# State-space phase: normed rows one batch ahead, inner products in the first pairs, softplus input earlier, row writes later

## The chip, the cores and the metric

The kernel runs on one core of one Trainium2 chip. The metric is the device time of one execution in microseconds, lower is better. The core's engines run their own instruction streams in order and meet through semaphores: PE (TensorE, matrix products; PEld are its weight loads), DVE (VectorE), ACT (ScalarE, functions from loaded tables), POOL (GpSimd), and SP, which issues transfers. TensorE's clock has two levels, 1.2 and 2.4 GHz; the profile gives the granted clock as a share of the full one.

## The reference

A two-layer decoder with residual blocks on x of shape (16, 256, 128). The change is in the first block only, which computes for each of the 16 sequences of 256 rows:

```python
xr = xn @ in_proj_w.T                       # xn: layer norm, then rms norm
xm, res = split(xr, 2)                      # 256 + 256 columns
u = silu(conv1d(xm, 4 taps) + conv_b)
dt, Bm, Cm = split(u @ x_proj_w.T, [8, 24]) # 8, 16 and 16 columns
delta = softplus(dt @ dt_proj_w.T + dt_proj_b)
h = exp(delta * A) * h + delta * Bm * u     # a scan over 256 rows, 16 states per channel
y = (einsum(h, Cm) + u * D) * silu(res)
x2 = rmsnorm(y @ out_proj_w.T + xn)         # then 8 experts, the best 2 for each row
```

Cross attention, a quantised feed-forward, and a second layer of the same kind of blocks follow; nothing in them changes.

## The kernel before, in words

`mamba` (L233) is one block with five instruction streams. Each of the 16 batches is one sequence of 256 rows (two groups of 128), and t counts the batches. The 16 states are taken in NP = 8 pairs p, and for each pair DVE does one scan for each half c of the 256 channels (L964) and then multiplies the states by the C rows (L973).

What a batch needs, in the order of the data:

- POOL `front` (L395): reciprocal deviations and scale factors of the rows. ACT `norm_in` (L503) makes h, ACT `unit` (L511) makes xn, PE `turn_in` (L743) turns xn into PSUM, ACT `turn_in` (L556) copies it to xnT. POOL `grow` (L426) adds h to the residual.
- PE `conv_in` (L751), twice, and `res_in` (L764): the in-projection with the four taps folded in, and the gate branch. ACT `front` (L561): silu of both, waiting first for the two convolutions and then for the gate branch.
- PE `dbl_out` (L772): the inner products that give dt, B and C. ACT `steps_out` (L571) copies them. PE `pre_out` (L782): dt to the width of delta.
- ACT `soft` (L580): softplus as max(x, 0) + log(1 + exp(-abs(x))): absolute value, exponential em, positive part. POOL `lost_part` (L418): the rounding that 1 + em loses. ACT `logarithm` (L594). POOL `steps_in` (L430): delta and du = delta * u. PE `turn_du` (L789), ACT `duT_in` (L620).
- `weigh` on three engines makes du * B for the states: POOL (L408) every even state, ACT (L598) the odd states of even pairs, DVE (L1017) the odd states of odd pairs. PE `feed` (L696) turns them into the scan's input. ACT `decays` (L608) makes exp(delta * A) of a pair.
- PE `spread` (L712) spreads the C rows of a pair over the partitions, `sums` (L733) adds the products, DVE `gate` (L975) multiplies with silu(res). PE `turn_y` (L798), ACT `yT_in` (L627), PE `carry` and `out` (L844, L807): the out-projection. ACT `size_out`, `store` (L520, L527), PE `turn_rows`, `gates` (L815, L825), ACT `rows_in`, `gates_in` (L535, L541): the normed output row and its gate logits. In batches 6, 10 and 14 DVE chooses experts (`choose`), and PE's `ranks` and DVE's `slots` follow in the next one; POOL's `sets` (L464) sends finished rows with indirect transfers from batch 7 on.

The order of work is written out by hand. Each engine has its own loop over t (POOL L473, ACT L642, PE L864, DVE L1028), and work for batch t + 1, and for the output of t - 1 and t - 2, stands between the pairs of batch t. PE does, for each pair p: a feed of pair p + 1, sums of p - 1, spread of p, sums, the second feed, and then what the loop lists for that p. xmP holds in turn the convolution, dt with B and C, softplus's input, and du turned; resP holds in turn xn turned, the gate branch, and y turned.

## Time and profile before

| | us |
|---|---|
| three timed runs | 2945.87, 2952.32, 2958.49 (median 2952.32) |
| the profiled execution | 2946.31, its span 2944.6 |
| PE busy in the span | 2435.7 (83%) |
| DVE busy | 1889.2 (64%) |
| ACT busy | 1669.0 (57%) |
| POOL busy | 1042.4 (35%) |
| state-space phase, scans of L964 | from 46.4, the last starts at 680.0 |
| granted clock over the span | 0.902 |

The span is one execution from its first to its last instruction. A row of the timeline is a run of like instructions of one engine with its start, its length, and in brackets how long the engine idled before it and who released it; a run overlaps the next one slightly, since instructions are pipelined. The share of busy time is a mean over phases with different limits.

### The profile page before, as it was taken

What the parts mean: (1) busy time and instruction counts of PE and PEld (TensorE: products, weight loads), DVE (VectorE), ACT (ScalarE), POOL (GpSimd) and SP (SyncE); (2) the same over time, 40 slices, a digit from 0 to 9 for tenths busy, and PEclk for the clock granted to TensorE, in tenths of its full rate; (3) what the DMA queues carried; (4) which work ended last, traced back from release to release, by engine and by line L of the source; (5) the groups of instructions that cost most, each with busy time, mean ns of one, the idle gap of its engine ahead of it and who ended that gap; (6) DMA issues with size and microseconds to landing.
All of it is one profiled execution on the core that took longest, in us unless ns stands there. A gap on an engine that the chain in (4) does not pass through costs nothing. (4 is left out here: it accounts for less than half of the span.)

```text
span 2944.6 us, 51871 instructions
## 1 busy us (share of the span) xinstructions
PE 2435.7 (83%) x17357; PEld 1874.4 (64%) x17359; DVE 1889.2 (64%) x3977; ACT 1669.0 (57%) x4651; POOL 1042.4 (35%) x1579
## 2 busy tenths in 40 slices
PE   5888788873995999998964896999998769989396
PEld 4777777763993666665642774666665547756385
DVE  5888777773224766666779453777776447767355
ACT  5777777771223777764554343877875346645011
POOL 4455564644451111102221312222220155523654
PEclk8998988886996999998985987999998979999598
DMA  8400000002652000000002100000000000000266
GB/s 344 191 1 1 8 8 5 12 1 89 192 174 73 2 1 1 2 1 7 1 8 47 24 1 18 1 1 2 1 2 9 9 9 1 1 9 14 88 204 198
DMA packets 73992, 130.00 MB, mean 44 GB/s; under 512 B 29113, under 2 KB 47361, under 8 KB 69634
## 3 DMA queue, kind: packets, MB, share of 16 engines
q1 hardware_dynamic: 62210, 103.46, 11.4%
q0 software_dynamic: 9216, 19.02, 1.8%
q10 hardware_dynamic: 2304, 4.20, 0.4%
q8 instruction: 143, 2.34, 0.3%
q14 instruction: 119, 0.97, 0.1%
HBM read 69.23 MB, written 57.41 MB: 43 GB/s over the span
## 5 line engine op out<-in xcount | busy, mean ns | idle before, releaser
L964 DVE TENSOR_TENSOR_SCAN s_state<-s_decay,s_inP 128x512 f32<-128x512 f32 x256 | 297.2, 1201 | 28.6 <-PE s_inP L708 15.3
L1890 ACT ACTIVATE s5a_prob<-s5a_scoreP,s5a_nmax 128x256 f32<-128x256 f32 x512 | 236.0, 482 | 22.6 <-DVE s5a_nmax L2070 21.0
L1890 ACT ACTIVATE s2s_prob<-s2s_scoreP,s2s_nmax 128x128 f32<-128x128 f32 (+1 forms) x512 | 208.6, 425 | 41.5 <-DVE s2s_nmax L2068 39.1
L708 PE MATMUL s_inP<-ident,s_wb 128*128 128x128 f32 x1024 | 174.3, 306 | 67.5 <-POOL s_wb L415 52.2
L617 ACT ACTIVATE s_decay<-s_delta,s_aneg 128x255 f32<-128x255 f32 x512 | 216.5, 496 | 3.7 <-POOL s_delta L434 3.4
L3651 POOL DMA_INDIRECT parts<-m_y,m_to x160 | 153.1, 957 | 134.6 <-DVE m_y L3742 109.5
L2070 DVE TENSOR_REDUCE s5a_nmax<-s5a_scoreP 128x4 f32<-128x1024 f32 x128 | 156.2, 1220 | 67.0 <-PE s5a_scoreP L1991 64.7
L708 PEld LDWEIGHTS s_inP<-ident,s_wb 128*128 128x128 f32 x1024 | 139.1, 161 | 78.7 <-issue 56.4
L973 DVE TENSOR_TENSOR s_state<-s_state,s_cP 128x512 f32<-128x512 f32 x256 | 162.0, 673 | 37.5 <-PE s_cP L720 37.5
L739 PE MATMUL s_ysumP<-ident,s_state 128*128 128x128 f32 x1024 | 164.7, 286 | 17.4 <-DVE s_state L973 17.4
L2068 DVE TENSOR_REDUCE s2s_nmax<-s2s_scoreP 128x2 f32<-128x256 f32 (+1 forms) x256 | 130.0, 550 | 76.1 <-PE s2s_scoreP L1986 73.6
L2081 DVE TENSOR_TENSOR s5a_probT<-s5a_probP,s5a_mask 128x768 f32<-128x768 f32 x128 | 122.5, 957 | 62.8 <-PE s5a_probP L2001 61.7
L2079 DVE COPY s2s_probT<-s2s_probP 128x768 f32<-128x768 f32 x128 | 122.6, 957 | 53.1 <-PE s2s_probP L2001 53.0
L3840 PE MATMUL m_hidP<-m_xT,m_w 128*128 128x256 f32 x640 | 155.3, 387 | 0.0
L1991 PE MATMUL s5a_scoreP<-s5a_k,s5a_q 32*128 32x256 f32 x1024 | 146.8, 404 | 0.8 <-ACT s5a_k L1870 0.8
L739 PEld LDWEIGHTS s_ysumP<-ident,s_state 128*128 128x128 f32 x1024 | 128.4, 149 | 22.1 <-DVE s_state L973 22.1
L415 POOL TENSOR_TENSOR s_wb<-s_duT,s_bct 128x512 f32<-128x512 f32 x128 | 132.1, 1060 | 15.7 <-ACT s_duT L625 15.3
L3840 PEld LDWEIGHTS m_hidP<-m_xT,m_w 128*128 128x128 f32 x640 | 118.2, 195 | 13.3
L3848 PEld LDWEIGHTS m_yP<-m_w,m_act 128*128 128x128 f32 x960 | 119.5, 192 | 4.7 <-DVE m_act L3734 0.7
L3848 PE MATMUL m_yP<-m_w,m_act 128*128 128x128 f32 x960 | 120.0, 275 | 0.5 <-DVE m_act L3734 0.5
L1986 PE MATMUL s2s_scoreP<-s2s_k,s2s_q 32*128 32x128 f32 (+1 forms) x1024 | 119.7, 352 | 0.0
L3798 ACT ACTIVATE m_act<-m_hidP 128x1024 f32<-128x1024 f32 x40 | 41.0, 1025 | 132.3 <-PE m_hidP L3840 132.3
(647 smaller groups left out, 6339.1 us busy)
## 6 DMA issues: line engine op xcount, KB each, us to landing
sorted<-blank SPq DMA_DIRECT2D x32, 1105.0 KB, 28.4
m_w<-in_m_w SPq DMA_DIRECT2D x40, 512.0 KB, 4.1
m_w<-in_m_w SPq DMA_DIRECT2D x40, 384.0 KB, 3.7
m_xin<-sorted SPq DMA_DIRECT2D x80, 130.0 KB, 2.5
m_back<-parts SPq DMA_DIRECT2D x16, 256.0 KB, 6.6
m_back<-parts ACTq DMA_DIRECT2D x16, 256.0 KB, 7.3
s4w_mats<-s_scratch SPq DMA_DIRECT2D x4, 1024.0 KB, 12.6
parts<-m_y,m_to POOLq DMA_INDIRECT x160, 3.3
```

The source lines that it names most:

```text
L415: ins = nc.gpsimd.tensor_tensor(wb[:, n, :, :], duT[:], bct[s][:, :, n:n + 1].to_broadcast([P, TB, 256]), ALU.mult)
L617: ins = nc.scalar.activation(decay[c][:, n, 1:], delta[:, c, 1:], ACT.Exp, scale=aneg[:, c, n:n + 1])
L708: ins = nc.tensor.transpose(inP[i % 3][:, a, g * P:(g + 1) * P], wb[:, k // 2 * 2 + a, g, c * P:(c + 1) * P], ident[:])
L739: ins = nc.tensor.matmul(ysumP[:, g, c * P:(c + 1) * P], state[r][:, c, a, g * P:(g + 1) * P], ident[:], start=False, stop=(p == NP - 1 an ...
L964: nc.vector.tensor_tensor_scan(flat(state[i % RING][:, c]), flat(decay[c][:, 2 * p:2 * p + 2, :]), flat(inP[(2 * i + c) % 3][:]), 0.0, ALU ...
L973: nc.vector.tensor_tensor(part, part, cP[:], ALU.mult).then_inc(S["prodded"], 1)
L1890: ins = nc.scalar.activation(prob[i][:, h, a:b], scoreP[i][:, h, a:b], ACT.Exp, bias=nmax[:, p % 4, h, r:r + 1], accum_out=den[s][:, r, 2 ...
L1991: ins = nc.tensor.matmul(scoreP[i][:, h, a:b], q[rows_of(h), c, r * P:r * P + P], k[rows_of(h), c, :], start=True, stop=True)
L2070: ins = nc.vector.tensor_reduce(nmax[:, p % 4, :, :].rearrange("p h r -> p (h r)"), scoreP[i][:].rearrange("p h (r k) -> p (h r) k", r=2), ...
L3651: nc.gpsimd.indirect_dma_start(acc, bass.IndirectOffsetOnAxis(to[s][:, i:i + 1], 0), y[s][:, i, :], None).then_inc(put[s], 16)
L3840: ins = nc.tensor.matmul(hidP[s % 2][:, c, :], w1[s][:, c, :], xT[s % 2][:], start=True, stop=True)
L3848: ins = nc.tensor.matmul(yP[s % 2][:, i * C:i * C + C], act[s % 2][:, k, i * P:i * P + P], w2[s][:, k, :], start=(k == 0), stop=(k == HK - 1))
```

## The change

It changes the order of the hand-written streams, a ring of buffers and two waits. Every operation of a batch stays, in number and size.

- The ring xn has 4 buffers where it had 3. ACT makes h and xn two batches ahead (in batch t for t + 2) and PE turns them then, after pair 5. Before, it was one batch ahead, in pairs 0 to 2.
- PE's convolutions of t + 1 stand behind pairs 0 and 1 (before 1 and 2), the gate branch and inner products behind 2 (before 3), the product for delta behind 3 (before 4), y's turning behind 3 (before 1), the rows' turning behind 6 (before 5).
- ACT's silu block stands behind the exponentials of pair 2 (before 5), the copy of dt, B and C behind the weighing for pair 4, softplus's first part behind the weighing for pair 6 (before behind the exponentials of pair 6). Row writes and the copy of y come after it.
- POOL's `front` stands behind its third weighing (before its eighth), and the addition of h, two of the row sends and the lost part stand between the eighth and delta.

```diff
-        xn = [sc.sb(f"xn{r}", [P, TB, C]) for r in range(3)]
+        xn = [sc.sb(f"xn{r}", [P, TB, C]) for r in range(4)]
             lost_part(0)
+            grow(1)
             steps_in(0, 0)
...
-                for p in range(4):
-                    weigh(t, s, p)
-                if more:
-                    grow(t + 1)
-                for p in range(4, 6):
-                    weigh(t, s, p)
-                if lot is not None and k < 3:
-                    sets(lot, 3 * k, 3 * k + 2)
-                for p in range(6, NP):
+                for p in range(3):
                     weigh(t, s, p)
                 if t + 2 < NB:
                     front(t + 2)
+                for p in range(3, NP):
+                    weigh(t, s, p)
                 if more:
                     lost_part(t + 1)
+                if t + 2 < NB:
+                    grow(t + 2)
+                if lot is not None and k < 3:
+                    sets(lot, 3 * k, 3 * k + 2)
+                if more:
                     steps_in(t + 1, 1 - s)
...
             def unit(t, s):
-                wait(ac, S["kept"], t - 2)
+                wait(ac, S["kept"], t - 3)
...
             soft(0)
+            norm_in(1)
+            unit(1, 1)
             logarithm(0)
+            turn_in(1)
             for t in range(NB):
                 decays(t, 0)
                 duT_in(t)
                 weigh(t, s, 0)
-                if more:
-                    norm_in(t + 1)
                 decays(t, 1)
-                if more:
-                    unit(t + 1, 1 - s)
                 weigh(t, s, 2)
                 decays(t, 2)
                 if more:
-                    turn_in(t + 1)
+                    front(t + 1, 1 - s)
                 decays(t, 3)
                 weigh(t, s, 4)
+                if more:
+                    steps_out(t + 1, 1 - s)
+                decays(t, 4)
+                weigh(t, s, 6)
+                if more:
+                    soft(t + 1)
                 if t >= 2:
                     store(t - 2)
                 if t >= 1:
                     yT_in(t - 1)
-                decays(t, 4)
-                weigh(t, s, 6)
                 decays(t, 5)
-                if more:
-                    front(t + 1, 1 - s)
-                    steps_out(t + 1, 1 - s)
+                if t + 2 < NB:
+                    norm_in(t + 2)
+                    unit(t + 2, s)
                 decays(t, 6)
                 if t >= 1:
                     size_out(t - 1)
-                if more:
-                    soft(t + 1)
+                if t + 2 < NB:
+                    turn_in(t + 2)
                 decays(t, 7)
...
             def res_in(t, s):
-                wait(pe, S["yT_ready"], t - 1)
+                wait(pe, S["yT_ready"], t - 2)
...
             def turn_y(t, above):
-                pe.wait_ge(S["xnT_ready"], above + 1)
+                pe.wait_ge(S["sres_ready"], above + 1)
...
                     if p == 0:
                         if more:
-                            turn_in(t + 1, 1 - s)
+                            conv_in(t + 1, 1 - s, 0)
                         skip(t, s)
...
                     elif p == 1:
                         if more:
-                            conv_in(t + 1, 1 - s, 0)
-                        if t > 0:
-                            turn_y(t - 1, min(t + 1, NB - 1))
+                            conv_in(t + 1, 1 - s, 1)
                     elif p == 2:
-                        if more:
-                            conv_in(t + 1, 1 - s, 1)
-                    elif p == 3:
                         if more:
                             res_in(t + 1, 1 - s)
                             dbl_out(t + 1, 1 - s)
-                    elif p == 4:
+                    elif p == 3:
                         if more:
                             pre_out(t + 1, 1 - s)
+                        if t > 0:
+                            turn_y(t - 1, min(t + 1, NB - 1))
+                    elif p == 4:
                         if t > 0:
                             carry(t - 1, 1 - s)
                             out(t - 1)
                     elif p == 5:
+                        if t + 2 < NB:
+                            turn_in(t + 2, s)
+                    elif p == 6:
                         if t >= 2:
                             turn_rows(t - 2)
```

## Rows read from the trace of the kernel before

**Rows 1.** Groups, 45 to 685 us: line, engine, tiles, count; busy, mean ns; idle before.

```profile
L964 DVE TENSOR_TENSOR_SCAN s_state<-s_decay,s_inP 128x512 f32<-128x512 f32 x256 | 297.2, 1201 | 28.6 <-PE s_inP L708 15.3 <-ACT s_decay L617 13.2
...
L973 DVE TENSOR_TENSOR s_state<-s_state,s_cP 128x512 f32<-128x512 f32 x256 | 162.0, 673 | 37.5 <-PE s_cP L720 37.5
...
L1024 DVE TENSOR_SCALAR s_wb<-s_duT,s_bct 128x256 f32<-128x256 f32 x127 | 53.8, 464 | 33.5 <-ACT s_duT L625 33.5
...
L980 DVE TENSOR_TENSOR s_yg<-s_ysumP,s_sres 128x512 f32<-128x512 f32 x16 | 11.1, 692 | 22.7 <-PE s_ysumP L739 22.7
```

**Rows 2.** Timeline of DVE, batch 5: start, length, line, tiles, count [idle before].

```profile
231.67 1.40 DVE L1024 TENSOR_SCALAR s_wb<-s_duT,s_bct 128x256 f32<-128x256 f32 x2 [1.82 <-ACT s_duT L625]
...
238.41 0.69 DVE L980 TENSOR_TENSOR s_yg<-s_ysumP,s_sres 128x512 f32<-128x512 f32 x1 [1.84 <-PE s_ysumP L739]
...
248.36 2.32 DVE L964 TENSOR_TENSOR_SCAN s_state<-s_decay,s_inP 128x512 f32<-128x512 f32 x2
...
255.47 1.28 DVE L973 TENSOR_TENSOR s_state<-s_state,s_cP 128x512 f32<-128x512 f32 x2 [1.37 <-PE s_cP L720]
...
260.25 1.29 DVE L973 TENSOR_TENSOR s_state<-s_state,s_cP 128x512 f32<-128x512 f32 x2 [0.72 <-PE s_cP L720]
```

**Rows 3.** Timeline of ACT, batch 5.

```profile
232.49 0.86 ACT L507 ACTIVATE s_h<-xres,s_shift,s_n_rstd 128x128 f32<-128x128 f32 x2
...
234.85 0.68 ACT L517 ACTIVATE s_xn<-s_h,s_rr 128x128 f32<-128x128 f32 x2
...
239.68 1.69 ACT L617 ACTIVATE s_decay<-s_delta,s_aneg 128x255 f32<-128x255 f32 x4
241.27 0.90 ACT L605 ACTIVATE s_wb<-s_duT,s_bct 128x256 f32<-128x256 f32 x2
...
245.12 0.60 ACT L631 ACTIVATE s_yT<-s_resP 128x512 f32<-128x512 f32 x1 [2.45 <-PE s_resP L804]
...
249.71 1.28 ACT L565 ACT_TABLE_LOAD   x1
251.01 0.84 ACT L565 ACTIVATE s_u<-s_xmP,s_convb 128x256 f32<-128x256 f32 x2
252.09 0.60 ACT L569 ACTIVATE s_sres<-s_resP 128x512 f32<-128x512 f32 x1 [0.24 <-PE s_resP L768]
...
259.38 0.84 ACT L586 ACTIVATE s_mag<-s_xmP,s_dtb 128x256 f32<-128x256 f32 x2
...
264.78 0.63 ACT L596 ACTIVATE s_lg<-s_em 128x512 f32<-128x512 f32 x1
...
269.58 0.57 ACT L625 ACTIVATE s_duT<-s_xmP 128x512 f32<-128x512 f32 x1
```

**Rows 4.** Timeline of PE, batch 5.

```profile
233.02 2.79 PE L708 MATMUL s_inP<-ident,s_wb 128*128 128x128 f32 x12 [2.42 <-POOL s_wb L415]
...
239.20 1.12 PE L729 MATMUL s_ysumP<-s_dd,s_u 128*128 128x128 f32 x8
...
242.27 0.66 PE L708 MATMUL s_inP<-ident,s_wb 128*128 128x128 f32 x4 [0.21 <-DVE s_state L964]
...
247.11 1.90 PE L759 MATMUL s_xmP<-s_xnT,s_wtap 128*128 128x256 f32 x8
...
251.02 1.03 PE L768 MATMUL s_resP<-s_win,s_xnT 128*128 128x256 f32 x4
...
256.17 1.12 PE L786 MATMUL s_xmP<-s_dtT,s_dtw 8*128 8x256 f32 x4
...
268.50 0.63 PE L795 MATMUL s_xmP<-ident,s_du 128*128 128x128 f32 x4 [2.06 <-POOL s_du L437]
```

**Rows 5.** Timeline of POOL, the end of batch 5.

```profile
265.74 1.26 POOL L434 TENSOR_TENSOR s_delta<-s_pos,s_lg 128x512 f32<-128x512 f32 x1
```

**Rows 6.** Stretches: length, busy us of PE, PEld, DVE, ACT, POOL, granted clock, transfers.

```profile
231.70:240.00 8.30, 6.98 (x37) 6.97 (x38) 5.29 (x7) 6.82 (x18) 8.28 (x9) 0.59 0.01 3
...
284.00:288.00 4.00, 4.00 (x18) 3.42 (x17) 4.00 (x5) 0.01 (x1) 0.00 (x0) 0.66 0.00 0
```

**Rows 7.** Timeline of PE, the first lull of batch 6.

```profile
283.64 1.11 PE L708 MATMUL s_inP<-ident,s_wb 128*128 128x128 f32 x4 [3.21 <-DVE s_state L964]
```

More of the change, by code:

```diff
@@ L514, in unit @@
                 wait(ac, S["turned"], t - 1)
-                wait(ac, S["kept"], t - 2)
+                wait(ac, S["kept"], t - 3)
                 for g in range(TB):
-                    ins = nc.scalar.activation(xn[t % 3][:, g, :], h[:, g, :], ACT.Copy, scale=rr[:, g:g + 1])
+                    ins = nc.scalar.activation(xn[t % 4][:, g, :], h[:, g, :], ACT.Copy, scale=rr[:, g:g + 1])
                 ins.then_inc(S["xn_ready"], 1)
@@ L747, in turn_in @@
                 for g in range(TB):
-                    ins = nc.tensor.transpose(turnP[:, g * P:(g + 1) * P], xn[t % 3][:, g, :], ident[:])
+                    ins = nc.tensor.transpose(turnP[:, g * P:(g + 1) * P], xn[t % 4][:, g, :], ident[:])
                 ins.then_inc(S["turned"], 1)
@@ L850, in carry @@
                 for g in range(TB):
-                    ins = nc.tensor.matmul(outP[:, g, :], ident[:], xn[t % 3][:, g, :], start=(g == 0), stop=False)
+                    ins = nc.tensor.matmul(outP[:, g, :], ident[:], xn[t % 4][:, g, :], start=(g == 0), stop=False)
                 ins.then_inc(S["kept"], 1)
@@ L859, in _ @@
             pre_out(0, 0)
+            turn_in(1, 1)
             turn_du(0)
```

## The prediction

> **What bounds the kernel now.** The change touches only the state-space phase, some 46 to 681 us of the span, 16 batches of about 38.5 us in a plain one. I read first the groups of that stretch with the idle time before each [rows 1]: DVE carries the recurrence (16 scans a batch), and what it idles for are outputs that wait for PE's spread C rows (37.5 us in all) and, once a batch, the first weighing, which waits for ACT's copy of duT (33.5 us). The scans and the gate add 28.6 and 22.7 us. So a batch is DVE's work plus about 7 us of idle. Then I read one plain batch, number 5, in order of time on each engine. Its zero is 231.63, where ACT has copied duT (the second such copy, 269.58 + 0.57, gives a period of 38.5) [rows 2, 3]. DVE idles 1.82 there, 1.2 before the first scan, 1.84 before the gate, and in the middle 1.37 and 0.72, where PE comes late with the spread of pairs 4 and 5 [rows 2]. ACT is far ahead in the middle: the exponentials of pair 3 run at 239.68, and their scan starts at 248.36 [rows 2, 3]. PE is the tight engine of the first pairs: its feed at 242.27 waited 0.21 us only [rows 4]. That reserve of ACT, some 7 us, is what the new order spends.
>
> **The change, part by part.** Nothing is computed that was not computed before; instructions change places. Times below are microseconds after the zero of the batch.
>
> *PE's first pairs.* The first convolution (8 matmuls; the group at 247.11 has 1.90, of which about 0.17 overlaps the next group: 1.73) moves from pair 1 to pair 0 and takes the place of the turning of xn (0.22, the skip products follow at 239.20) [rows 4]. So PE reaches the feed in front of the second convolution about 1.3 us later (1.5 less the 0.21 of waiting): the convolution in pair 1 starts at 12.4 and not 11.1, and ends at 14.1. Pair 2 then runs feed, sums, spread, sums, feed, five groups of 0.43, to 16.3. DVE's pair 1 is not late: its spread ends at 11.5, and its scans end at about 11.6.
>
> *ACT's front.* It stood after the exponentials of pair 5 and now stands before those of pair 3, as one block: silu of u, silu of the gate branch, and the next exponential needs its table back. The table for silu (1.28) is loaded while ACT waits. The gate branch is copied 1.07 after the start of its product (251.02 to 252.09) [rows 3, 4], so at 17.4. The copy takes 0.5, the table 1.30 (249.71 to 251.01 shows the step) [rows 3]: the exponentials start at 19.2, the first two are done at 20.0. DVE was ready for the scan of pair 3 at 16.7 [rows 2]. That is a new idle of about 3.2 us where there was none.
>
> The Trainium skill's ScalarE: Activation LUTs, section What ACT_TABLE_LOAD costs, asks about 2.66 us for each change of table, a drain included. The row has 1.28 and the next activation 0.02 behind it, so the trace does not show that drain here, and the sum goes by the row; by the page this one step would be 1.4 us a batch dearer.
>
> *The feed behind it.* ACT's weighing for pair 4 follows the exponentials of pair 3 (1.6, then 0.9) and is done at 21.7. Before, it was done at 10.5 (241.27) [rows 3]. PE's feed of pair 4 waits for it at the head of pair 3. Behind that feed are queued the sums of pair 2 and the spread of pair 3, on which DVE's outputs of pair 3 wait. PE is through with the gate product and the inner products at 19.1 (three groups like the 1.03 at 251.02, less their overlaps: 2.8), so it idles 2.6 us. The spread ends at 23.0; DVE's scans of pair 3 end at 22.3, so it idles 0.7 more. Then PE has the product that widens dt (1.05, the group at 256.17) at 23.9 to 24.9 [rows 4]. In the old order it ended at 25.6, so softplus's input comes only 0.7 us earlier, not a pair earlier.
>
> *From softplus to the next batch on ACT.* In the new order everything between is a chain without waits: softplus 2.1 (259.38 and what follows it), yT 0.5, exponentials of pair 5 1.6, h and xn 0.8 + 0.6, pair 6 1.6, pair 7 1.6, table 1.3, logarithm 0.6 [rows 3], and four small ones (row write, sizes, xnT, rowT), which I price by the copy of yT and below it, 0.45 each: 12.5 us, so the logarithm is done at 37.4. It was done at 33.8 (264.78 + 0.63 less the zero). DVE, let go at pair 5 by its exponentials (28.9, the end of its first two), does scans and outputs 5, 6 and 7 at 3.45 each and ends at 39.3. From the logarithm the tail is the old one: delta and du on POOL 1.3 each, turning 0.7, duT 0.6 with hops: 4.0, so 41.4. POOL's three steps of the lost part, 4.6 us, leave this tail, but they ended only some 0.2 us behind the logarithm (delta starts at 265.74, the logarithm ends at 265.41) [rows 3, 5], so moving them is worth 0.2 us at the most. The new wait of y's turning (for the gate branch's silu, done at 17.9) is met when PE comes to it at 24.9, and the turning of xn at 31.2 finds xn made at 31.1. Row writes and the turnings on PE count nothing beyond the chain above, since DVE is still busy; if not, each costs its own 0.2 to 0.6.
>
> *Sum without a change of clock.* Period 41.4 against 38.5: +2.9. Check by DVE's idle: +3.2 and +0.7 new; 1.37 and 0.72 gone, for which 0.3 and 0.6 come back (pair 4 behind the moved turning of y, pair 5 behind its exponentials); boundary 1.8 to 2.1; this gives +3.0. Plain batches 0 to 5: 6 x 2.9 = 17.4. Batches 6, 10 and 14 have the choice of experts on DVE (4 us), which hides the new ACT wait: +0.2 each. Batches 7 and 11 put the rank products (some 2 us of PE) into pair 0 beside the moved convolution, where there is no backlog to spare, and start with a clock that rises a little sooner: +3.5 each. Batches 8, 9, 12 and 13: 2.9 plus 0.25, because POOL's sends stand between du and the next weighing: 12.6. Batch 15 has no next batch: 0. The prologue has POOL's addition of h (0.7) before delta. Together 17.4 + 0.6 + 7.0 + 12.6 + 0.7 = 38 us.
>
> *PE's clock.* The new 2.6 us lull comes in the middle of busy PE. Before, the lull of 3.21 us before 283.64 was followed by a granted clock of 0.66 for 284 to 288 (part of it at the lower level, 1.2 of 2.4 GHz), and four transposes took 1.11 there, 0.66 at 242.27 [rows 4, 6, 7]. Two more batches with a choice show lulls of 3.3 to 3.5 us. At the batch's start, where the lulls are 2.06 and 2.42 us with 0.6 of work between (the first at 268.50, the second at 233.02; one such pair at each of the plain starts), the stretch 231.7 to 240 has 0.59 [rows 4, 6]. So 2.6 us alone is between a case that always falls and gaps of 1 us that never do; I take it to fall in about two batches of three. Price: PE is the critical engine from the feed to the product for delta (3.4 us of work at the full level, twice that at the lower). A short fall, as at 283.64, costs half its length of 3.4 us, 1.7; a long one, as at the starts, the whole 3.0; mean 2.1 us. Bounds: nothing in 15 batches, or 3.0 in all, 45 us. Value: ten to fourteen batches x 2.1, I take 26.
>
> The Trainium skill's TensorE: Matmul & The Clock Gate, section HAM oscillation — how this bites in real kernels, describes a wait of PE that returns in every iteration and lets the clock fall each time; by it all 15 batches would pay, about 31 us for my 26.
>
> The profiled execution took 2946.3 us (span 2944.6), at the low end of the three timed ones (2945.9 to 2958.5, median 2952.3). Its own time plus 38 plus 26 is 3010 us. I leave it there; measured from the median it would be 6 us more.
>
> **The rivals.**
> *A, the clock holds.* The same new waits, no fall: 2946 + 38 = 2984. For it: 2.6 us is shorter than the 3.21 that fell. Against: the pair of lulls at each start falls every time.
> *B, faster: the relief of pairs 4 and 5 decides.* If ACT gets its front's inputs before DVE needs pair 3, only the removal of PE's late spreads stays: 2.09 us x 15 = 31, so 2915. It decides at the time of the gate product: it would have to start by 13.0 (DVE's 16.7 less 1.07, 0.5, 1.3 and 0.85 for the first two exponentials), and it stands behind a feed that needs the first scan of pair 2, which DVE finishes at 14.0, and 0.43 for the feed. So even a PE with no backlog misses it by 1.4 us; only a shorter hop or table would help.
> *C, the waits only change places.* What pair 3 costs, pairs 4 and 5 and the tail give back, if the chain from softplus had slack that I do not see (2.9 us): 2950.
> *D, every lull falls long.* 2946 + 38 + 45 = 3029. The longer boundary lull (about 2.9 before the turning of du where it was 2.06) [rows 4] speaks for it.
>
> **How the numbers follow.** Forecast 0.58 (own range 2992 to 3024), A 0.22, D 0.06, B 0.08, C 0.06. The predicted time is 3010. The range runs from A's lower side to D, 2970 to 3034, and leaves out B, C and a little at the top. What this kernel's measurement can tell is about 0.5%, 15 us. Slower by more: forecast, A, D = 0.86; B gives faster 0.08, C within 0.06.
>
> **What would show it.** Right: DVE's scans of pair 3 wait about 3 us for ACT's exponentials in each of batches 0 to 5; ACT idles some 7 us before its first silu; PE idles about 2.6 us before the feed of pair 4, released by ACT's weighing; four transposes behind it take about 1.1 us; POOL's part step no longer stands before delta; a plain period is 41 to 44 us. Wrong: a period of 38.5 or less; silu of the gate branch finished before 16; a clock of 1.0 behind the lull (then A); a logarithm done before 36.

## The result and the profile after

The changed kernel takes 3033.73 us (3021.62 to 3042.58) beside 2951.79 for the kernel before: ratio 1.027, 95% interval 1.022 to 1.033. One of its four runs (3071.77, granted clock 0.879) fell in a slower state that some executions of any kernel here show, and the medians and ratios of this document leave such runs out. The change is slower, as forecast, by 24 us more than the 3010 named; the time lies inside the range of 2970 to 3034, by less than 1 us. The execution profiled is the longest of the three (3042.58): its span is 3040.8 us, 96 more than before.

Where the 96 us lie is read from the first and last load of m_xin, with which the expert phase begins and ends. The first one is issued at 733.8 us before and at 819.9 after: the state-space phase, with what is left of it behind the last batch, costs 86 us. From the first to the last load it is 2164.2 before and 2174.6 after, though nothing there was changed. The twelve profiles of the experiments scatter there: 2161.6 to 2173.4 in x1 to x7, 2183.5 to 2194.9 in x8 to x12, whose executions of before were also some 30 to 40 us longer. So I count these 10 us as no part of the change, and below I compare the ends of the state-space phase ("phase end", always the first load of m_xin) beside the ratios.

The groups of the changed kernel from 45 to 785 us (line, engine, tiles, count, busy, mean ns, idle before):

```profile
L969 DVE TENSOR_TENSOR_SCAN s_state<-s_decay,s_inP 128x512 f32<-128x512 f32 x256 | 297.3, 1201 | 61.3 <-ACT s_decay L617 46.9 <-PE s_inP L711 14.3
...
L978 DVE TENSOR_TENSOR s_state<-s_state,s_cP 128x512 f32<-128x512 f32 x256 | 161.9, 672 | 57.5 <-PE s_cP L723 57.4
...
L1029 DVE TENSOR_SCALAR s_wb<-s_duT,s_bct 128x256 f32<-128x256 f32 x128 | 83.3, 691 | 49.6 <-ACT s_duT L625 49.6
```

Against [rows 1] DVE's scans have the same 1201 ns, but DVE idles 33 us more ahead of them, all of it for ACT's exponentials. Ahead of the outputs it idles 20 more, and the weighings themselves are 30 us dearer (691 ns for 464). The wait ahead of the first weighing of each batch has hardly grown: of the 49.6 us, 13.8 are the wait of the very first one, which begins at 44.73 and is not among the 127 of [rows 1], so that like for like it is 35.9 for 33.5. So some 50 us of the loss are waits, and 30 are longer weighings.

Batch 5 of the changed kernel begins at 261.47 (duT copied), and the next at 307.05: 45.6 us for 38.5. DVE in it (start, length, line, tiles, count, idle before):

```profile
269.59 2.26 DVE L1029 TENSOR_SCALAR s_wb<-s_duT,s_bct 128x256 f32<-128x256 f32 x2
...
278.61 0.60 DVE L1029 TENSOR_SCALAR s_wb<-s_duT,s_bct 128x256 f32<-128x256 f32 x2
281.35 2.33 DVE L969 TENSOR_TENSOR_SCAN s_state<-s_decay,s_inP 128x512 f32<-128x512 f32 x2 [2.14 <-ACT s_decay L617]
284.87 1.28 DVE L978 TENSOR_TENSOR s_state<-s_state,s_cP 128x512 f32<-128x512 f32 x2 [1.19 <-PE s_cP L723]
...
292.18 1.28 DVE L978 TENSOR_TENSOR s_state<-s_state,s_cP 128x512 f32<-128x512 f32 x2 [3.79 <-PE s_cP L723]
...
307.08 1.40 DVE L1029 TENSOR_SCALAR s_wb<-s_duT,s_bct 128x256 f32<-128x256 f32 x2 [1.82 <-ACT s_duT L625]
```

ACT in the same batch:

```profile
266.41 1.28 ACT L565 ACT_TABLE_LOAD   x1
275.46 0.84 ACT L565 ACTIVATE s_u<-s_xmP,s_convb 128x256 f32<-128x256 f32 x2 [7.76 <-PE s_xmP L762]
278.51 0.60 ACT L569 ACTIVATE s_sres<-s_resP 128x512 f32<-128x512 f32 x1 [2.21 <-PE s_resP L771]
279.12 1.28 ACT L617 ACT_TABLE_LOAD   x1
280.42 1.70 ACT L617 ACTIVATE s_decay<-s_delta,s_aneg 128x255 f32<-128x255 f32 x4
282.02 0.89 ACT L605 ACTIVATE s_wb<-s_duT,s_bct 128x256 f32<-128x256 f32 x2
...
288.51 0.84 ACT L586 ACTIVATE s_mag<-s_xmP,s_dtb 128x256 f32<-128x256 f32 x2 [2.84 <-PE s_xmP L789]
...
302.22 0.63 ACT L596 ACTIVATE s_lg<-s_em 128x512 f32<-128x512 f32 x1
```

And PE, with the granted clock of stretches of 4 us behind it (length, busy of PE, PEld, DVE, ACT, POOL, clock, transfers):

```profile
277.44 1.03 PE L771 MATMUL s_resP<-s_win,s_xnT 128*128 128x256 f32 x4
...
279.36 1.08 PE L781 MATMUL s_xmP<-s_xp_bc,s_u 128*128 128x32 f32 x8
283.06 0.63 PE L711 MATMUL s_inP<-ident,s_wb 128*128 128x128 f32 x4 [2.62 <-ACT s_wb L605]
...
286.40 2.07 PE L789 MATMUL s_xmP<-s_dtT,s_dtw 8*128 8x256 f32 x4
```

```profile
280.00:284.00 4.00, 1.38 (x13) 1.30 (x13) 2.33 (x2) 3.99 (x12) 0.00 (x0) 1.00 0.00 0
284.00:288.00 4.00, 4.00 (x18) 3.23 (x15) 3.13 (x4) 1.67 (x5) 0.00 (x0) 0.53 0.01 4
288.00:292.00 4.00, 4.00 (x19) 3.60 (x18) 0.40 (x1) 3.46 (x9) 1.90 (x1) 0.50 0.00 0
292.00:296.00 4.00, 4.00 (x28) 4.00 (x27) 3.82 (x5) 3.92 (x12) 3.45 (x4) 0.69 0.00 0
```

These rows show one event spread over three engines. ACT waits for the convolution and for the gate product (7.76 and 2.21), changes its table, and only then has the exponentials for which DVE stands 2.14. PE stands 2.62 for ACT's weighing. A few instructions later the granted clock is at its lower level, 1.2 of 2.4 GHz, and stays there for about 10 us. In them the product that widens dt takes 2.07 where it took 1.12 in [rows 4], and DVE stands 3.79 for the spread of pair 4.

### The profile page after: what moved, and what is told of

It is laid out like the page before. It is cut to its first block and busy times, and to the rows that moved or that the text cites. A ratio compares the mean times of both kernels' runs of the same rounds, so it can differ in the third digit from the quotient of the medians.

```text
span 3040.8 us, 51871 instructions
## 1 busy us (share of the span) xinstructions
PE 2490.7 (82%) x17359; PEld 1909.6 (63%) x17359; DVE 1924.2 (63%) x3977; ACT 1668.6 (55%) x4651; POOL 1045.3 (34%) x1579
## 5 line engine op out<-in xcount | busy, mean ns | idle before, releaser
L969 DVE TENSOR_TENSOR_SCAN s_state<-s_decay,s_inP 128x512 f32<-128x512 f32 x256 | 297.3, 1201 | 61.3 <-ACT s_decay L617 46.9
L711 PE MATMUL s_inP<-ident,s_wb 128*128 128x128 f32 x1024 | 185.6, 320 | 107.6 <-POOL s_wb L415 47.6
L742 PE MATMUL s_ysumP<-ident,s_state 128*128 128x128 f32 x1024 | 175.3, 299 | 14.9 <-DVE s_state L978 14.9
L742 PEld LDWEIGHTS s_ysumP<-ident,s_state 128*128 128x128 f32 x1024 | 137.2, 157 | 21.2 <-DVE s_state L978 21.2
L415 POOL TENSOR_TENSOR s_wb<-s_duT,s_bct 128x512 f32<-128x512 f32 x128 | 132.9, 1070 | 15.1 <-ACT s_duT L625 13.8
L421 POOL TENSOR_SCALAR s_part<-s_em 128x512 f32<-128x512 f32 x16 | 31.0, 1939 | 269.3 <-ACT s_em L589 269.3
```

What stands on the lines that cost most here:

```text
L415: ins = nc.gpsimd.tensor_tensor(wb[:, n, :, :], duT[:], bct[s][:, :, n:n + 1].to_broadcast([P, TB, 256]), ALU.mult)
L711: ins = nc.tensor.transpose(inP[i % 3][:, a, g * P:(g + 1) * P], wb[:, k // 2 * 2 + a, g, c * P:(c + 1) * P], ident[:])
L742: ins = nc.tensor.matmul(ysumP[:, g, c * P:(c + 1) * P], state[r][:, c, a, g * P:(g + 1) * P], ident[:], start=False, stop=(p == NP - 1 an ...
L969: nc.vector.tensor_tensor_scan(flat(state[i % RING][:, c]), flat(decay[c][:, 2 * p:2 * p + 2, :]), flat(inP[(2 * i + c) % 3][:]), 0.0, ALU ...
```

## The experiments

Two theories of the loss. **Theory 1:** ACT's block with both silus, put in front of pair 3's exponentials, is the cause: directly by its waits, and through the lull of PE and the lower clock behind it. **Theory 2:** POOL's new places are the cause: its scale factors for the batch after next stand between its third and fourth weighing, so that its later weighings run beside DVE's, its part of softplus stands beside another weighing of DVE's, and DVE's weighings are slowed. Five runs (x1 to x5) tell these apart, the other seven ask what bounds the batch once they are gone. Where single batches are compared, a batch is taken from one copy of duT to the next.

**x1, the silu block moved back by one pair.**

```
                 decays(t, 2)
-                if more:
-                    front(t + 1, 1 - s)
                 decays(t, 3)
                 weigh(t, s, 4)
                 if more:
+                    front(t + 1, 1 - s)
                     steps_out(t + 1, 1 - s)
```

> The changed kernel with one block moved on ACT: the silu block of the next batch stands behind the exponentials of pair 3 and the weighing for pair 4, not before them. Theory 1 (the place of this block starts the new waits, PE's lull of 2.6 us behind the inner products and the fall of the clock after it): DVE's scans of pair 3 no longer wait (2.14 us a batch in the changed kernel), PE's feed of pair 4 no longer waits 2.6 us, the clock no longer falls in mid batch; 15 batches x about 4 us less, so about 2975 us, and a plain batch of 39 to 41 us. Rival (PE's new order alone, the convolution in pair 0 and the turnings behind pairs 5 and 6, makes it slow): the time stays above 3020 us.

2970.54 us, ratio 1.0074 (1.0056 to 1.0093), phase end 752.0: 68 of the 86 us are gone with one block moved by four exponentials and a weighing. The granted clock no longer falls behind the inner products in any batch of its trace. DVE in x1:

```profile
247.22 1.80 DVE L1028 TENSOR_SCALAR s_wb<-s_duT,s_bct 128x256 f32<-128x256 f32 x2
...
266.04 2.33 DVE L968 TENSOR_TENSOR_SCAN s_state<-s_decay,s_inP 128x512 f32<-128x512 f32 x2 [1.20 <-ACT s_decay L617]
...
279.11 1.40 DVE L1028 TENSOR_SCALAR s_wb<-s_duT,s_bct 128x256 f32<-128x256 f32 x2 [2.73 <-ACT s_duT L625]
```

The weighing for pair 3 (247.22) still takes three times as long as the next one (0.60 at 255.77), and the wait at the end of the batch has grown from 1.82 to 2.73.

**x2, POOL's steps behind its eighth weighing, all else as changed.**

```
-                for p in range(3):
+                for p in range(NP):
                     weigh(t, s, p)
                 if t + 2 < NB:
                     front(t + 2)
-                for p in range(3, NP):
-                    weigh(t, s, p)
```

> The changed kernel with POOL's scale factors for t + 2 made behind its eighth weighing, as before the change, and not between the third and the fourth. Theory 2 (DVE's weighing for pair 3 takes 2.0 us in the changed kernel and not 0.6 to 0.8, because it now runs beside a POOL weighing, and that lengthens the batch by itself): 15 x 1.3 us less, about 3018 us. Theory 1: DVE waits for ACT two pairs later anyway, so the weighing gets short again but the time falls by 0 to 8 us, 3030 to 3038.

3034.22 us, 1.0292 (1.0279 to 1.0305), phase end 820.4: nothing in sum. In the plain batches 0 to 5 a shorter weighing ends in a longer wait, while DVE stands for ACT and PE further down the batch (0.5 us more in all six together). Batch by batch the sum hides two effects: batches 6 and 10 are 3.5 and 3.6 us shorter, and batches 8 and 12 are 3.7 and 3.8 longer, because in these two the granted clock now falls behind the lull of 2.62, which it did not in the changed kernel.

**x4, both moves** (the two diffs above together).

> The changed kernel with both moves of the first two experiments. Theory 1 with theory 2 as the next limit: without the wait for ACT, DVE paces the batch, and the shorter weighing for pair 3 counts in full: 10 to 19 us less than the move of the silu block alone, about 2960 us. If DVE does not pace it then (PE or ACT does): the same as with the silu block alone, within 5 us.

2953.85 us, 1.0022 (1.0011 to 1.0033), phase end 742.8. The same POOL move that was worth nothing in sum is now worth 9 us of phase (17 in the medians). The weighing that took 1.80 in x1 beside POOL's weighings, and what POOL does beside it now:

```profile
246.26 0.61 DVE L1026 TENSOR_SCALAR s_wb<-s_duT,s_bct 128x256 f32<-128x256 f32 x2
```

```profile
245.98 0.71 POOL L398 TENSOR_TENSOR s_n_rstd<-s_var,s_n_power 128x2 f32<-128x2 f32 x1
```

But the shorter weighing is not what pays most. Of the 9.8 us in the batches 7.6 lie in 6, 10 and 14, where DVE chooses experts. In the other twelve the weighings are 10.6 us shorter in all, and 7.1 us of that come back as waits ahead of the outputs, for PE's spread. In x1, as in the changed kernel, some steps of the choice run beside POOL's weighings and take four times as long; the first row is of the changed kernel, the second of x4:

```profile
315.34 0.97 DVE L1000 SCALAR_TENSOR_TENSOR s_conv<-s_conv,s_col 128x64 f32<-128x64 f32 x1
```

```profile
286.29 0.23 DVE L997 SCALAR_TENSOR_TENSOR s_conv<-s_conv,s_col 128x64 f32<-128x64 f32 x1
```

The whole choice takes 5.33 and 4.57 us in batches 6 and 10 of x1, and 3.66 and 3.74 in x4. PE's lull behind it shrinks with it, from 4.08 and 2.95 to 2.40 and 2.48, and the clock, which fell behind the lull in x1, holds. So theory 2's mechanism is real and a tenth of the loss, but most of it comes through the batches with a choice. The Trainium skill, SBUF — State Buffer, section Terms, says that DVE and GpSimd arbitrate for one pair of ports, and that an instruction holds it to its end. The rows agree in direction for the weighing (1.80 beside POOL's weighings, 0.61 beside its small scale-factor steps); DVE's scans keep their 1201 ns beside the same weighings.

**x3 and x5, the lull of PE filled.** x3 computes the products for B and C three times instead of once (32 columns wide, into the same place). x5 puts eight products without use, 128 wide, into a place that is written afterwards. x3, then x5:

```
+                for again in range(3):
+                    for g in range(TB):
+                        for c in range(2):
+                            ins = nc.tensor.matmul(bctP[:, g, :], ...)
```

```
                     nc.tensor.matmul(dtP, xp_dt[:, c, :], u[s][:, c, :], start=(c == 0), stop=(c == 1))
+                keep_busy(nc, xmP[:, 0, P:2 * P], ident, 8)
```

> The changed kernel with the B and C products of each batch computed three times over into the same place, so that PE works 1.8 us longer behind the inner products, in time in which it idled for 2.6 us. Nothing waits longer for it, since ACT copies them 1.8 us later at the earliest. If the lull lets the clock fall: the granted clock behind it stays at 1.0, four transposes there take 0.6 and not 1.06 us, and the time falls by the half of the 78 us of added low clock or a little less, 25 to 39 us, to about 3005. If the clock falls for another reason, or its fall costs nothing: 3038, or some us more.

> The changed kernel with eight products of the identity with itself (128 x 128, some 1.9 us) between the dt product and the B and C products, into a part of xmP that is not read. The third experiment filled the same lull with narrow products (32 columns), and the clock fell all the same behind a lull of 0.84 us. If narrow products keep the clock up less than wide ones: the granted clock stays at 1.0 behind the lull, and the time falls by 20 to 35 us below the 3026 us of the third experiment or, from the changed kernel's 3038, by 25 to 39. If what lies before the lull does not matter and 0.8 us of idle time is enough: 3025 as in the third experiment.

x3: 3026.7 us, 1.0262 (1.0246 to 1.0277), phase end 810.0. It missed: the lull was 0.84, and in batch 5 the clock fell all the same.

```profile
273.50 2.87 PE L782 MATMUL s_xmP<-s_xp_bc,s_u 128*128 128x32 f32 x24
277.20 0.63 PE L711 MATMUL s_inP<-ident,s_wb 128*128 128x128 f32 x4 [0.84 <-ACT s_wb L605]
277.67 0.88 PE L742 MATMUL s_ysumP<-ident,s_state 128*128 128x128 f32 x4
278.34 1.06 PE L723 MATMUL s_cP<-ident,s_bct 128*128 128x128 f32 x4
```

x5: 2998.82 us, 1.0155 (1.0109 to 1.0200), phase end 786.2. The lull is the same 0.83, and four transposes behind it take 0.60:

```profile
269.73 0.63 PE L711 MATMUL s_inP<-ident,s_wb 128*128 128x128 f32 x4 [0.83 <-ACT s_wb L605]
270.20 0.60 PE L742 MATMUL s_ysumP<-ident,s_state 128*128 128x128 f32 x4
```

The granted clock from 120 to 680 us: first the changed kernel, then x3, then x5 (before has 0.90).

```profile
120.00:680.00 560.00, 438.00 (x2843) 384.28 (x2841) 420.30 (x536) 374.75 (x857) 268.64 (x322) 0.85 0.02 5
```

```profile
120.00:680.00 560.00, 457.48 (x3083) 401.02 (x3084) 427.63 (x545) 383.96 (x881) 277.06 (x333) 0.88 0.02 5
```

```profile
120.00:680.00 560.00, 452.87 (x3192) 396.40 (x3192) 441.29 (x571) 388.73 (x892) 277.59 (x334) 0.92 0.02 5
```

So the clock is worth 34 us of phase end (35 of the medians). Nearly all of it (34.2 of 35.9 us in the batches) lies in the eleven batches in which the changed kernel's clock fell behind this lull, 3.1 us for each. With the narrow products the clock fell behind it in nine batches (it held in 2 and 3), with the wide ones in none. The wait for ACT's exponentials stays in x5 (2.15 in batch 5), as it should. The Trainium skill, TensorE: Matmul & The Clock Gate, section HAM oscillation — how this bites in real kernels, describes a kernel in which PE waits some 3 to 5 us in every iteration and the clock falls in each. Here the wait is shorter, 2.62 us, and the clock fell behind it in eleven batches of fifteen. In the batches 8, 9, 12 and 13 it held: the same lull of 2.62 stands before 429.37, and the transposes behind it take 0.60. The prediction read the page as if all 15 would pay.

**x6 and x7, the end of the batch.** x6 is the kernel before with three small moves on ACT: softplus ahead of the sums of squares, the logarithm ahead of the copy of the output row, and the gate logits of the batch one later. x7 has the second and third in x4, and there softplus behind the exponentials of pair 5. The edit of x6:

```
                 weigh(t, s, 0)
+                if t >= 3:
+                    gates_in(t - 3)
...
                 decays(t, 6)
-                if t >= 1:
-                    size_out(t - 1)
                 if more:
                     soft(t + 1)
+                if t >= 1:
+                    size_out(t - 1)
                 decays(t, 7)
-                if t >= 2:
-                    rows_in(t - 2)
                 if more:
                     logarithm(t + 1)
                 if t >= 2:
+                    rows_in(t - 2)
+                if t == NB - 1:
                     gates_in(t - 2)
```

> The kernel before, with three moves on ACT alone: softplus's first part before the squares of the output rows (which wait for PE's out-projection), the logarithm before the copy of the turned rows, and the copy of the gate logits one batch later, behind the first weighing. Theory (the tail from softplus's input through the logarithm, delta, du and duT sets the gap between two batches; the changed kernel moved em but left the logarithm behind the copy of the rows): em and the logarithm come 1.9 us earlier, DVE's wait of 1.82 us before its first weighing goes nearly to 0, 15 x 1.8 = 27 us less than before, about 2922. Rival (the tail is set elsewhere, by PE's turning of du behind the gate products or by the scan's feed): 2945 to 2952.

> The fourth experiment (silu block behind the weighing for pair 4, POOL's scale factors behind its eighth weighing) with four more moves on ACT: the exponentials of pair 5 before softplus's first part and behind the copy of y, the logarithm before the copy of the turned rows, and the copy of the gate logits one batch later. In the fourth experiment a batch still has 1.2 us of waiting for the exponentials of pair 5, 1.0 us of PE for the copy of y, and 2.7 us before the first weighing. Theory: 1.2 of the first and some 0.9 of the last go, 15 x 2.1 = 31 us less than the fourth experiment's 2955, about 2925. Rival (PE's load in pairs 0 to 2 with the clock at its lower level sets the batch): not below 2945.

x6: 2914.20 us, 0.9929 (0.9889 to 0.9969; the two medians alone give 0.988), phase end 699.2: faster than both kernels. DVE no longer stands at the end of a plain batch (5.8 us in all ahead of its weighings, for 33.5 in [rows 1]), its weighing starts on time (and is then 1.87 long, beside POOL's). Ahead of the scans and of the gate it idles 8 and 7 us less. In pair 4 it stands as before:

```profile
243.38 1.28 DVE L975 TENSOR_TENSOR s_state<-s_state,s_cP 128x512 f32<-128x512 f32 x2 [1.38 <-PE s_cP L722]
...
256.19 1.87 DVE L1026 TENSOR_SCALAR s_wb<-s_duT,s_bct 128x256 f32<-128x256 f32 x2
```

x7 missed: 2964.44 us, 1.0058 (1.0044 to 1.0072), phase end 751.0, worse than x4. The plain batches are a little better (2 to 5 take 156.3 us, 157.6 in x4), those from 7 on worse (43.9 for 41.4 in batch 7), for a reason that x9 shows below: in batches 7, 8, 9, 11, 12 and 13 delta starts 2.3 to 2.5 us behind the logarithm, behind POOL's row sends, and in all others 0.08. Batch 5 shows why the order of the small copies gains little there: from the table load in front of the exponentials of pair 4 (254.70) to the end of the logarithm (270.62) ACT never idles. It is 15.9 us of work in a row, in which the change has put h and xn of the batch after next (1.57) between softplus and the logarithm. That gave the third theory: **in the new order a plain batch is as long as ACT's chain.**

**x8 and x9, h and xn taken out of that chain.** x8 is x4, and x9 is x7, with

```
                 weigh(t, s, 4)
+                if t + 2 < NB:
+                    norm_in(t + 2)
+                    unit(t + 2, s)
                 if more:
                     front(t + 1, 1 - s)
...
                 decays(t, 5)
-                if t + 2 < NB:
-                    norm_in(t + 2)
-                    unit(t + 2, s)
```

and x10 is x6 again.

> This is x4_both_moves with one more move: ACT makes h and xn of the batch after next (s_h, s_xn; 1.57 us) in its wait for the convolution (5.26 us in the trace of x4), and no longer between softplus and the logarithm. Theory 1 (what keeps the new order slower than before is ACT's unbroken chain from the gate branch's silu to the logarithm, which the change made longer by the rows of the batch after next): the logarithm comes about 1.6 us earlier in each of 14 batches, the boundary wait of DVE falls from 2.7 to about 1.1, the time from 2955 to 2930 to 2936. Theory 2 (the boundary is held by something else, the turning of xn or the gates on PE's queue ahead of du, or POOL): unchanged, 2950 to 2958.

> This is x7_change_repaired with the same one move (s_h and s_xn before the silu block). Theory 1: the chain is shorter by 1.6 us, and the waits of x7 at scan 6 (0.88) and most of the boundary's 2.75 go with it; 2964 becomes 2938 to 2944 if x7's 9 us above x4 stay, 2925 to 2932 if the wait at scan 6 was their cause. Theory 2: unchanged, 2960 to 2966.

> x6_before_tail_shorter again, on the same chip as the two others, to compare with them: 2912 to 2922, 1% faster than before. If its gain was chance, 2945 to 2955.

Beside these three the kernel before took 2977.94 us, so only ratios are compared: x8 1.0014 (1.0000 to 1.0027), x9 1.0006 (0.9994 to 1.0018), x10 0.9900 (0.9868 to 0.9932). x10 confirms x6. x8 and x9 gained less than expected (0.1% on x4, which is not clear of the intervals, and 0.5% on x7). In x9 the plain batches did what the theory says: four of them (2 to 5) take 149.9 us, 156.3 in x7 and 153.8 before, so 1.6 us less for each. In x8 they take 155.2 for 157.6 in x4, 0.6 each where 1.6 was expected, and DVE's wait at the end of batch 5 fell from 2.72 to 1.82 and not to 1.1: ACT now stands 0.81 for PE's turning of the row in front of the logarithm. What failed in x9 are the batches from 7 on: batch 9 has 43.5 us in x9, where batch 5 has 37.5 and batch 9 of the kernel before 40.0. POOL shows it, in x9:

```profile
383.23 0.73 POOL L428 TENSOR_TENSOR xres<-xres,s_h 128x256 f32<-128x256 f32 x1
384.12 1.10 POOL L230 DMA_INDIRECT sorted<-m1r_first,m1r_idx  x1 [0.17 <-issue]
385.53 0.96 POOL L230 DMA_INDIRECT sorted<-m1r_second,m1r_idx  x1 [0.30 <-issue]
386.80 0.95 POOL L230 DMA_INDIRECT sorted<-m1r_first,m1r_idx  x1 [0.30 <-issue]
388.06 0.96 POOL L230 DMA_INDIRECT sorted<-m1r_second,m1r_idx  x1 [0.30 <-issue]
389.04 1.27 POOL L434 TENSOR_TENSOR s_delta<-s_pos,s_lg 128x512 f32<-128x512 f32 x1
```

The logarithm was done at 385.16. The row sends, which the change moved from between the weighings to here, hold delta by 3.9 us.

**x11 and x12, the row sends moved out of the tail**, in x9 and in the changed kernel:

```
+                if lot is not None and k < 3:
+                    sets(lot, 3 * k, 3 * k + 2)
                 if more:
                     lost_part(t + 1)
                 if t + 2 < NB:
                     grow(t + 2)
-                if lot is not None and k < 3:
-                    sets(lot, 3 * k, 3 * k + 2)
```

> This is x9_units_and_soft_moved with POOL's four sends of expert rows (sorted <- m1r_first, m1r_second; 5.1 us in batches 7, 8, 9, 11, 12 and 13) put before its wait for softplus's exponential (14.8 us long in the trace of x9), where x9, like the change, has them right ahead of delta. Theory 1 (x8 and x9 shortened ACT's chain, and in those six batches POOL's sends became what delta waits for: they end at 389.04 where the logarithm is done at 385.16): delta comes 3.8 us earlier in six batches, 23 us in all; the ratio to before falls from 1.0006 to 0.992 or 0.993. Theory 2 (the long batches 7 to 13 come from PE's clock or from the choice of experts, not from POOL): ratio 0.999 to 1.002.

> This is the changed kernel with the same one move of the sends. In its own trace delta waits 0.81 to 0.97 us for the logarithm behind the sends, so they are hidden by ACT's late chain. Theory 1: nothing, within 0.2% of the changed kernel (ratio to before 1.025 to 1.030). Theory 2 (the sends ahead of delta are part of the change's loss): 5 us in six batches, 30 us, ratio 1.017 or lower.

x11: ratio 0.9920 (0.9903 to 0.9936), as expected. The sends run in POOL's idle time, and delta waits for ACT again:

```profile
360.02 1.09 POOL L230 DMA_INDIRECT sorted<-m1r_first,m1r_idx  x1 [0.29 <-issue]
...
381.44 1.26 POOL L434 TENSOR_TENSOR s_delta<-s_pos,s_lg 128x512 f32<-128x512 f32 x1 [1.28 <-ACT s_lg L594]
```

x12: 1.0252 (1.0236 to 1.0269), inside the band of no effect: in the changed kernel ACT's chain is so late that it covers the sends, and delta starts 0.08 us behind the logarithm in every batch but the first, with the sends in either place. The new order can be made faster than the kernel before, by 0.8% with seven moves; the old order is as good with three (x6 and x10, 0.7% and 1.0%).

## Why the prediction was right, and too low

The direction, the place and the two mechanisms (ACT's block, and the clock behind PE's lull) were right, and the size was too low: 64 us forecast (38 without the clock, 26 of clock), 82 measured in the medians and 86 in the phase of the profiled executions. That the time still lies in the range is luck in part. The top of the range stood for a clock that falls long in every batch, which did not come; the time got there because other terms were too small. A plain batch was to take 41 to 44 us, and the six took 40.9 to 46.9.

| step, batch 5 (us after its zero) | forecast | measured |
|---|---|---|
| gate product starts | 16.3 | 16.0 |
| table for the exponentials loaded, they start | 19.2 | 18.95 |
| DVE's new wait for them | 3.2 | 2.14 |
| lull of PE before the feed of pair 4 | 2.6 | 2.62 |
| softplus starts | 24.9 | 27.0 |
| softplus to the end of the logarithm | 12.5 | 14.3 |
| logarithm to duT copied | 4.0 | 4.2 |
| period | 41.4, with a clock fall 43.5 | 45.6 |

**The new waits.** Right in place and cause. DVE's was 1.1 shorter than forecast, because DVE itself came later to pair 3 (at 17.7 and not 16.7): its weighing for pair 3 (269.59), in front of the scans of pair 1, took 2.26, for 0.87 before.

**The step that was wrong: "Batches 6, 10 and 14 have the choice of experts on DVE (4 us), which hides the new ACT wait: +0.2 each."** Against before they are 8.5, 7.1 and 5.1 us longer (batch 6: 54.06 for 45.53); with two more for a clock fall, 7 had been forecast in all and 20.7 came, so 14 of the 22 us that were missing lie in these three. The choice stands ahead of the scans of pair 1, for which PE's feed in front of the second convolution waits, so the silu of u comes later by as much as DVE does, and nothing is hidden. Two things come on top: in batches 6 and 10 the choice itself takes 5.35 and 5.26 us for 3.35 and 3.63 before, beside POOL's weighings (x4 takes that away), and the granted clock then stays at its lower level for 13.7 us. Batch 6 of the changed kernel, PE, ACT and DVE:

```profile
321.64 1.05 PE L711 MATMUL s_inP<-ident,s_wb 128*128 128x128 f32 x4 [4.10 <-DVE s_state L969]
```

```profile
325.75 0.84 ACT L565 ACTIVATE s_u<-s_xmP,s_convb 128x256 f32<-128x256 f32 x2 [12.47 <-PE s_xmP L762]
```

```profile
331.64 2.33 DVE L969 TENSOR_TENSOR_SCAN s_state<-s_decay,s_inP 128x512 f32<-128x512 f32 x2 [2.71 <-ACT s_decay L617]
```

I had taken the wait for a fixed time on ACT, when it is a link that returns to DVE. x5, where the lull of 2.62 costs no clock, tests the sum without the clock, group by group (us above the kernel before):

| batches | forecast | x5 |
|---|---|---|
| 0 to 5, plain | 17.4 | 18.0 |
| 6, 10 and 14, with a choice | 0.6 | 7.1 |
| 7 and 11, with rank products | 7.0 | 7.9 |
| 8, 9, 12 and 13 | 12.6 | 16.1 |

The agreement of the first row is better than its terms deserve: it left out the longer weighings, and had DVE's new wait too long.

**The clock, a term that was mis-sized.** 26 us forecast, 34 measured (x5). The number of falls was right: ten to fourteen forecast, eleven came, and batches 8, 9, 12 and 13 kept the clock. Each fall costs 3.1 us and not 2.1. In batches 0, 1, 4, 7 and 11 the low stretch lasts 3.4 us, in the six others 10.2 or 13.7. In batch 5 (10.2) it takes in the dt product, through which it delays softplus (27.0 for 24.9) and so the whole tail, not only the spread.

**The chain from softplus.** 12.5 us forecast without waits, 12.9 measured in batch 8 with the clock held (432.84 to 445.71), 14.3 in batch 5, where ACT stands 0.97 and 0.61 for the turnings of xn and of the row. I had written that these count nothing; after a clock fall they do. I named this chain as what ends the batch, and x9 bears that out for the plain batches, but did not draw what follows from it: that h and xn in it cost 1.6 us a batch once the silu block is put right and nothing else is in the way. x8 got a third of that.

**The weighings.** Not in the sum at all. They grew by 30 us on DVE. In x4 they are 10 us shorter than in x1, of which 7 come back as waits (see x4): most of what x4 gains, it gains in the batches with a choice.

**The row sends.** The sends that the change puts ahead of delta have no term in the forecast. That was right for the changed kernel (x12), and would be wrong once ACT's chain is shorter, as in x7 and x9 (x11 against x9: 0.9%).

Taking the phase ends in turn, the 86 us are: 34 of clock (819.9 to 786.2, x5), 34 of ACT's late block (786.2 to 752.0, x1, which has neither), 9 of POOL's weighings beside DVE's choice and its weighings (752.0 to 742.8, x4), and 9 of ACT's longer chain and what else is in the new order (742.8 to 733.8). The order of taking away matters, as x2 shows, and each phase end is of one profiled execution.

**The rivals.** A (the clock holds, 2984) is the kernel x5, which took 2999: even then the waits were 14 us dearer than my 38, half of it in the batches with a choice (3.9, 2.6 and 0.6 longer than before, for 0.2 each). B and C fell: the waits for the late spreads of pairs 4 and 5 did shrink, to 0.30 and nothing in batch 8, but pair 3 now waits 0.98 for its own, and ACT's waits outweigh it. D (3029) is the nearest number, 5 us short, and not the mechanism: four lulls kept the clock and five falls were short.

What stays open: why the same lull of 2.62 lets the clock fall in batch 5 and not in batch 8 (in x2 it fell in batch 8 too), what the last 9 us of the new order are made of, and the scatter of 10 us in the expert phase.

## What to carry to other kernels

Before an operation is moved ahead of another on an in-order engine, ask when its own inputs come. ACT had 7 us in reserve for its own work, and none for a block that waits for PE, which waits for DVE: a reserve is spent by waiting, not by working.

A term that is priced at nothing because something hides it holds only as long as that cover stands still. The places of POOL's scale factors and of its row sends cost nothing in the sum of the changed kernel, and 0.5% (x4 against x1) and 0.9% (x11 against x9) in repaired ones; so a part should be undone once alone and once with the largest cause already gone. And a sum of nothing should be read batch by batch: in x2 it was a gain of some 7 us in two batches and a loss of as much in two others.

Where the trace has a wait of 2 us at the end of every batch, moving three small operations out of the way of the logarithm gave as much (0.7% and 1.0%) as the rearranged phase did after seven repairs (0.8%).

## What the runs showed of the hardware

A lull of PE that was filled up to 0.84 us with products of 32 columns let the granted clock fall in nine batches of fifteen (0.73 and 0.84 in the two stretches of 4 us from 276 in x3); filled to 0.83 with products of 128 columns it held at 1.00 in all. The same lull of 2.62 us let it fall in eleven batches of the changed kernel and not in four.

A pair of DVE's weighings takes 0.60 us alone, 1.4 to 2.3 beside POOL's weighings (128x512) and 1.63 beside its addition to s_pos, but still 0.61 beside its scale-factor steps (128x2, x4); some steps of DVE's choice take 0.97 for 0.22 beside the same weighings. Scans beside them keep their 1201 ns.

A table load of ACT starts while the instruction behind it still waits for its input (266.41 for a silu at 275.46), so the load in front of a silu costs nothing when PE is late; only the load back, 1.28 us at 279.12, stands in the chain.
